# Image normalisation one step further ahead, a reordered filling, and one cast of the second feed-forward pass moved to GpSimd

## The reference

```python
x = x + _L0_conv_ref(_gn(x), ...)      # group norm, then 2 of 4 experts per pixel: 96 -> 96 (ReLU) -> 96
t = _to_tokens(x)                      # [32, 784, 96]
t = t + _L1_attn_ref(_ln_t(t), ...)    # linear attention over the 784 tokens of an image
t = t + _L1_ffn_ref(_ln_t(t), ...)     # two layers with sign weights, 96 -> 384 -> 96
x = _from_tokens(t, x)

def _quantize_activations_groupwise(x):          # after each layer of the feed-forward part
    for g in range(5):                           # 5 groups of 6 images; images 30 and 31 give zero
        gamma = jnp.max(jnp.abs(ag))             # one maximum over a whole group
        xq = xq.at[...].set(jnp.clip(ag * QB / (gamma + EPS), -QB + EPS, QB - EPS))
```

## Time and profile before

| | |
|---|---|
| median of 3 executions | 816.02 us (815.99 to 819.28) |
| profiled execution | 814.42 us, of which the span of its instructions 812.6 us |
| TensorE, VectorE, ScalarE, GpSimd busy | 748.0, 632.2, 480.2, 270.4 us of the span |
| granted TensorE clock, mean | 0.973 |

### The profile page before, as it was taken

The page is one execution under the profiler, slowest core; times in us unless marked ns, Lnnn a source line. Parts: engine busy times, 40 slices in busy tenths (PEclk is TensorE's granted clock), DMA queues, the critical chain, the costliest instruction groups (busy, mean ns, idle before and its releaser), DMA issues.

```text
span 812.6 us, 14931 instructions
## 1 busy us (share of the span) xinstructions
PE 748.0 (92%) x4624; PEld 496.5 (61%) x4624; DVE 632.2 (78%) x1735; ACT 480.2 (59%) x684; POOL 270.4 (33%) x449
## 2 busy tenths in 40 slices
PE   6698699999999999999999999999997799999991
PEld 3465456767667776677776677766766355555540
DVE  3577457788888887887888878888876478998997
ACT  2455445656546565455565565654642599988981
POOL 1350133543544544445445355354443000000000
PEclk9799899999999999999999999999997999999996
DMA  9880012211112212122111121111100101653343
GB/s 219 186 198 15 17 45 59 57 51 57 47 44 59 59 44 59 44 59 59 44 59 44 46 60 56 47 57 30 44 16 16 44 1 60 165 163 117 119 119 119
DMA packets 23489, 57.09 MB, mean 70 GB/s; under 512 B 5385, under 2 KB 5671, under 8 KB 23463
## 3 DMA queue, kind: packets, MB, share of 16 engines
q1 hardware_dynamic: 23064, 56.15, 25.4%
q10 hardware_dynamic: 399, 0.60, 0.3%
HBM read 37.94 MB, written 18.67 MB: 70 GB/s over the span
## 4 chain that ended last, share of the span: by engine, by line
PE 43%; DVE 25%; issue 7%; POOL 6%; ACT 4%; DVEq 1%; ACTq 0%; POOLq 0%
PE slot L1047 10%; DVE tok L1491 10%; PE slot L1104 9%; PE slot L915 6%; POOL ln_rs L643 5%; PE slot L1070 5%; PE slot L1073 5%; PE slot L1242 4%; DVE ln_st L1481 4%; DVE stage L1615 3%; DVE ln_mv L1485 2%; PE slot L1280 2%; PE slot L1284 1%; ACT hT L869 1%; DVE y2max L1622 1%
## 5 line engine op out<-in xcount | busy, mean ns | idle before, releaser
L1063 PE MATMUL slot<-hT,w2s 128*96 128x392 f32 x384 | 141.7, 492 | 0.0
L1497 DVE TENSOR_REDUCE ymax<-slot 128x784 f32 (+1 forms) x90 | 87.1, 972 | 41.0 <-PE slot L1073 40.3
L828 ACT COPY xh1T<-slot 96x784 f32<-96x784 f32 x32 | 25.8, 807 | 157.0 <-PE slot L915 157.0
L797 ACT ACTIVATE hT<-slot,b1c,w_unit 128x784 f32<-128x784 f32 x96 | 96.1, 1004 | 35.6 <-PE slot L1047 35.5
L637 POOL TENSOR_TENSOR ln_ve<-ln_mv,ln_eps 112x7 f32<-112x7 f32 x62 | 12.6, 203 | 303.0 <-DVE ln_mv L1485 303.0
L1491 DVE TENSOR_SCALAR tok<-tok,ln_mv,ln_rs 112x96 f32<-112x96 f32 x224 | 96.8, 500 | 15.7 <-POOL ln_rs L643 15.7
L643 POOL TENSOR_TENSOR ln_rs<-ln_ve,pow_half 112x7 f32<-112x7 f32 x62 | 92.7, 1496 | 2.5
L1070 PE MATMUL slot<-big,W1b 99*128 (+1 forms) x360 | 90.0, 331 | 2.5 <-DVE ymax L1497 1.3
L869 ACT ACTIVATE hT<-slot,s 128x784 f32<-128x784 f32 x90 | 80.4, 929 | 16.0 <-PE slot L1073 9.1
L1073 PE MATMUL slot<-big,W1b 96*128 (+1 forms) x360 | 89.6, 329 | 0.0
L650 POOL TENSOR_SCALAR tok<-tok,ln_nm,ln_rs 112x96 f32<-112x96 f32 x210 | 84.9, 420 | 9.2 <-POOL ln_rs L643 9.2
(11 more groups left out here) (190 smaller groups left out, 1348.6 us busy)
## 6 DMA issues: line engine op xcount, KB each, us to landing
out<-t2T SPq DMA_DIRECT2D x56, 294.0 KB, 2.6
xr<-in_x SPq DMA_DIRECT2D x32, 294.0 KB, 2.9
big<-in_x SPq DMA_DIRECT2D x7, 1176.0 KB, 15.4
xs<-in_x SPq DMA_DIRECT2D x28, 294.0 KB, 2.9
xs<-out SPq DMA_DIRECT2D x24, 294.0 KB, 3.3
big<-out SPq DMA_DIRECT2D x1, 1764.0 KB, 11.0
out<-big SPq DMA_DIRECT2D x6, 294.0 KB, 2.6
big<-in_x SPq DMA_DIRECT2D x2, 588.0 KB, 25.1
```

The costliest lines, as they stand in the source:

```text
L797: nc.scalar.activation(hT[q][:, t, :].rearrange("p (a n) -> p a n", a=2), halves(k, P), ACT.Relu, scale=w1_unit[:, t:t + 1], bias=b1c[:, t ...
L1063: ins = mm(S[k][0:C, h, 0:HALF], w2s[:, v, t, :], hT[q][:, t, h * HALF:(h + 1) * HALF], start=t == first, stop=t == last, skip_group_check ...
L1497: V.tensor_reduce(ymax[:, bass.ds(3 * f + t, 1)], halves(k, P), AX.XY, ALU.max, apply_absolute_value=True).then_inc(ymax_done[t], 1)
```

## The change

It has three parts. `LAG_NORM` becomes -1: step i normalises image i + 1, and ScalarE does it after the copy of R instead of at the step's start; GpSimd's `xn_rest` and SP's load follow the same lag, and the first and last steps are adapted. In the filling, the first attention's x1 stands behind the first two hidden tiles on TensorE, image 2 is normalised before the filling's first step, and `first_shares(1)` and `first_weights(1)` move behind VectorE's steps 3 and 5. In the second pass GpSimd makes `h_hi` of tile 1, and ScalarE only that of tile 0; the semaphore `hi_parts` becomes two.

```diff
-        LAG_NORM = LAG_HID = 0
+        LAG_NORM = -1
+        LAG_HID = 0
...
+            def gelu_part(b, r):
+                wait_apart(pool, gelu_ready, 3 * b + 2, pool_passed)
+                if not (isinstance(b, int) and b < 2):
+                    wait_apart(pool, y2_ready, b - 1, pool_passed)
+                nc.gpsimd.tensor_copy(h_hi[r][:, 1, :], gel[:, 1, :]).then_inc(hi_parts[1], 1)
+
+            for r in range(2):
+                gelu_part(r, r)
+            with pool.Fori(1, QIMAGES // 2) as m:
+                for r in range(2):
+                    gelu_part(2 * m + r, r)
...
-                if exists(hid) and not (isinstance(hid, int) and hid < 2):
-                    norm_image(m, r)
+                norm, _, _ = at(m, r, LAG_NORM)
...
                     nc.scalar.copy(R[:, :], S[3][0:C + 1, 0, 0:C]).then_inc(r_ready, 1)
+                if exists(norm) and not (isinstance(norm, int) and norm <= 2):
+                    norm_image(m, r)
                 if exists(att):
...
             relu(1, 1, 2, 0)
+            norm_image(0, 1)
             act.wait_ge(signs_ready, 1)
...
-                if i == 2:
+                if i == 4:
                     gate_exps(1, 1)
...
-                nc.scalar.copy(h_hi[r][:, t, :], gel[:, t, :]).then_inc(hi_parts, 1)
+                nc.scalar.copy(h_hi[r][:, t, :], gel[:, t, :]).then_inc(hi_parts[0], 1)
...
                     gelu_tile(g, b, 2)
-                    gelu_hi(b, 1, r)
...
+                first_attention = isinstance(att, int) and att == 0
+                if exists(att) and not first_attention:
+                    x1_channels()
...
                     hidden(1, 3, hid_q)
+                if first_attention:
+                    x1_channels()
...
-            step(0, 1)
-            first_shares(1)
-            step(1, 0)
-            step(1, 1)
-            first_weights(1)
-            for i in range(4, EVEN_FIRST):
+            for i in range(1, EVEN_FIRST):
                 step(i // 2, i % 2)
+                if i == 3:
+                    first_shares(1)
+                if i == 5:
+                    first_weights(1)
...
-                    dve.wait_ge(hi_parts, SPLIT * b + t + 1)
+                    dve.wait_ge(hi_parts[t], b + 1)
```

More of the change, by code:

```diff
@@ L414, in build @@
         qv_ready = sem("qv_ready")
-        hi_parts = sem("hi_parts")
+        hi_parts = [sem(f"hi_parts{t}") for t in range(2)]
         o_ready = sem("o_ready")
@@ L514, in _ @@
                 step(i // 2, i % 2)
-            with sp.Fori(EVEN_FIRST // 2, BATCH // 2 - 1) as m:
+            with sp.Fori(EVEN_FIRST // 2, BATCH // 2 - 2) as m:
                 for r in range(2):
                     step(m, r)
-            for i in range(BATCH - 2, DRAIN):
+            for i in range(BATCH - 4, DRAIN):
                 step(i // 2, i % 2)
@@ L667, in _ @@
                 step(i // 2, i % 2)
-            with pool.Fori(EVEN_FIRST // 2, BATCH // 2) as m:
+            with pool.Fori(EVEN_FIRST // 2, BATCH // 2 - 1) as m:
                 for r in range(2):
                     step(m, r)
-            for i in range(BATCH, DRAIN):
+            for i in range(BATCH - 2, DRAIN):
                 step(i // 2, i % 2)
+            def gelu_part(b, r):
[8 more added lines that the diff above has]
+                    gelu_part(2 * m + r, r)
         @block.scalar
@@ L855, in _ @@
                 step(i // 2, i % 2)
-                if i == 2:
+                if i == 4:
                     gate_exps(1, 1)
-            with act.Fori(EVEN_FIRST // 2, BATCH // 2) as m:
+            with act.Fori(EVEN_FIRST // 2, BATCH // 2 - 1) as m:
                 for r in range(2):
                     step(m, r)
-            for i in range(BATCH, DRAIN):
+            for i in range(BATCH - 2, DRAIN):
                 step(i // 2, i % 2)
@@ L1192, in step, with x1_channels @@
                     mix(1, 1, mix_q, 0, 2, 0).then_inc(y_mixed, 1)
-                if exists(att):
+                def x1_channels():
                     if filling:
@@ L1206, in step @@
                     wait_count(pe, tok2_ready, tok2_image + 1)
+                    if first_attention:
+                        pe.wait_ge(tok1_ready, 1)
                     hidden(0, 2, hid_q)
                     wait_count(pe, t2_ready, done + 1)
-                    if isinstance(hid, int) and hid == 2:
+                    if first_attention:
                         pe.wait_ge(gate_exp_in, 3)
                     hidden(1, 3, hid_q)
+                if first_attention:
+                    x1_channels()
                 if exists(att):
```

## The result

The changed kernel took 823.88 us as the median of 20 executions (818.87 to 828.81), the kernel before 816.00 in 20 beside them (814.22 to 820.83); the ratio over undisturbed executions is 1.0074, with a 95% interval of 1.0055 to 1.0093. By this ratio it is 6 us slower, by the two medians 7.9; the interval lies wholly above 1, and the time is outside the range of the prediction. The profiled execution took 818.99, 4.6 over the profiled 814.42 of before; it was one of the quickest of its kernel, 4.9 under the median, where that of before was 1.6 under.

A forecast was written before the change was run, and what follows sets the result against it. TensorE was taken to bound the main loop, with waits for VectorE's late apply, and three engines within 5% the later second pass. A -4.8, B -1.0 and C +4.5 sum to -1.3: from 816.0 to 814.7 us, range 807 to 822.

The forecast's parts named there:

- B: Filling: earlier statistics and first x1, against later Am of steps 4 and 6; -1.0 us in sum, bounds -3.5 to +0.5.
- A: Main loop: normalising one step ahead makes xn_rest start behind the apply's last instruction, ending TensorE's wait; -4.8 us.
- C: Second pass: moving one tile's cast from ScalarE to GpSimd relieves ScalarE but holds VectorE; net +4.5 us.
- C, the first image and four group starts: Second pass: VectorE no longer waits for ScalarE's second cast there, about 0.6 us each; -3.0 us.
- C, the other images: Second pass: GpSimd's cast holds VectorE's clip for 0.5 us in each of 15 images; +7.5 us.
- the main loop's collision stays: Rival: xn_rest's request falls ahead of the apply's seventh start, so the loop gains only 0.2 us; 819.3 us, chance 0.20.
- the exponential: Filling: the feature map's exponential starts 4.1 us earlier, taken as -3.7 after allowing for the clock.
- +1.8 as forecast: Filling: `first_shares(1)` now stands ahead of the Am of step 4 and delays it; +1.8 us.
- +1.2 against +0.9: Filling: `first_weights(1)` now stands ahead of the Am of step 6 and delays it; +0.9 us.
- priced at 0.4: Filling: a clock fall in the remaining waits costs x1, keys and values up to 1.5 us more; 0.4 taken.
- The rival's 820.7: Second pass: cast waits behind the clip, addition and splits, delaying the second split 0.9 us an image; heavy-cast rivals together 0.20.

The follow-up runs named there:

- experiments 9 and 10: The changed kernel with one and with two GpSimd semaphore instructions ahead of xn_rest: 809.74 us (ratio 0.9888) and 812.72 us (0.9916).
- experiment 2: The changed kernel with one wait more, GpSimd starting xn_rest only when VectorE's apply of that step is done: 803.51 us, ratio 0.9830.
- experiment 7: The changed kernel once more, unchanged, beside the kernel before: 824.89 us, ratio 1.0090.

## Why the prediction was wrong

The forecast was a small gain, to 814.7, with a range of 807 to 822; the kernel became slower, 823.88. Of the sum, by the starts of Am and `y2_out` in the two profiles:

| term | predicted | measured |
|---|---|---|
| B, the filling (to the Am of step 6) | -1.0 | -1.0 |
| A, main loop (to the last Am) | -4.8 | +2.5 |
| C, the first image and four group starts | -3.0 | -1.3 - 2.1 = -3.4 |
| C, the other images | +7.5 | +6.5 |
| sum | -1.3 | +4.6 |

**A failed**, at "So the request of GpSimd comes just behind the last start, by 0.08 us. I take it that the apply then takes 1.77". The start was forecast well (0.02 to 0.07 behind the seventh's start instead of 0.08), but the boundary was the wrong one: not that start, but 0.07 to 0.12 behind it (experiments 9 and 10). It was missed by 0.1 us or less, and it decided some 12 us. Even the forecast 0.08 lies where no run tells the side. The rival "the main loop's collision stays" was the true case, with a chance of 0.20, and was itself too mild: it let the collision cost nothing, since "the chain then waits as long as now". But the apply now first runs six instructions and then waits through all of xn_rest, 1.48 + 1.67 + 0.07 = 3.22, where before xn_rest had begun 0.06 ahead of it: 3.11. A step went from 17.14 to 17.26 on the mean, by these 0.11.

**What A could have won** was too small as well: 0.38 in each of 25 steps (17.14 - 16.76), 9.5 us, not 5.05. The 0.16 of experiment 2, by which the idle time shown ahead of x1 seems short, would make most of the difference.

**B was right in the first profile**, term by term: the exponential -4.0 against -3.7, then +1.8 as forecast and +1.2 against +0.9. For the median it failed in one term. That the clock may fall behind the shorter wait was priced at 0.4; of eight profiled executions five show it, at 1.7 to 4.6, and three don't (experiment 7). That the first profile agrees with B is luck in this.

**C had the right size by the wrong instruction**, which is luck. The place and the price were of the clip, held by the cast for 0.5. In truth the clip, 0.09 to 0.15 ahead of the cast, holds the cast, and the addition is held for 0.32 and 0.52. That the addition would be held is what the prediction had read from the Trainium skill ("SBUF — State Buffer", "Who interferes with whom"); I gave it only the rival's chance because no row of before showed it. The rival's 820.7 put the price on a split that comes late by the cast's whole length, and in these images it did not. The cast is 0.84, against the 0.9 taken.

**From the profile to the median** the prediction added the 1.6 of before. For the changed kernel it is 4.9; experiment 7 shows one cause, the clock in the filling. Whether that is all of it is open, since most executions have no profile. From 814.7 to 823.88 it is 9.2: 5.9 of it lie in the profiles (A came out 7.3 worse, C 1.4 better), and 3.3 lie here.

## What to carry to other kernels

Where a forecast rests on a tie of 0.1 us that repeats in every step, it is two forecasts: price both sides and put the chance near even, or take the tie away, as one more wait did here (20 us). When moving an instruction past another that shares a lock with it, ask for its place among the single instructions of the other group, and let it start clearly behind the last of them; starting ahead held the apply too, for 1.34 in the kernel before. Work that is given to GpSimd should lie beside VectorE instructions that the trace shows running at their own length beside it; here that was the maximum, and choosing the other tile was enough.

## What was not expected of the hardware

- The start of a VectorE row doesn't show that the instruction has the lock. One that started 0.04 us ahead of GpSimd's was held 1.45 by it; with GpSimd 0.10 later it was not held at all. Nor does the end of a row show until when it has the lock: GpSimd went on some 0.15 ahead of it (experiments 9 and 10).
- The lock works both ways: a clip of 0.61 kept GpSimd's cast (0.84 to 1.22) and even its plain write (0.75 to 1.22) waiting, while an addition with two inputs was held by the cast and not by the write, and a maximum was not held by the cast.
- TensorE's idle time in the rows ahead of x1 was some 0.16 a step shorter than the time lost there, on the mean of the loop (0.34 shown, 0.50 lost); that an overlap with the row before makes this is worked out from the rows and not tested.
- Of eight executions in which TensorE waited 1.8 us at the same place, five show a fall of the granted clock right behind it and three none.
